# A transformer layer on one core: values of two blocks by seven block products, rope sums partly on GpSimd

## The reference

```python
qkv = x @ w_qkv.T                      # 4096 x 512 by 512 x 1536
q, k, v = split(qkv)                   # 16 heads of 32
q = q * cos + rotate_half(q) * sin
k = k * cos + rotate_half(k) * sin
scores = q @ k.T * 32 ** -0.5          # keep 0 <= row - column < 64
x = layernorm(x + softmax(scores) @ v @ w_out.T)
gate = silu((x @ w_gate) * s_gate)
up = (x @ w_up) * s_up
x = layernorm(x + ((gate * up) @ w_down) * s_down)
```

## Time and profile before

| | |
|---|---|
| median of three runs | 1167.06 (1166.32 to 1167.65) |
| the profiled execution | 1166.03 |
| its span, first to last instruction | 1164.2 |
| PE busy | 1154.0 (99%) |
| DVE busy | 984.6 (85%) |
| ACT busy | 584.4 (50%) |
| POOL busy | 587.3 (50%) |
| DMA: packets, MB | 352077, 134.80 |
| granted TensorE clock | 1.000 of full speed |

### The profile page before, as it was taken

The page is one execution under the profiler, slowest core; times in us unless marked ns, Lnnn a source line. Parts: engine busy times, 40 slices in busy tenths (PEclk is TensorE's granted clock), DMA queues, the critical chain, the costliest instruction groups (busy, mean ns, idle before and its releaser), DMA issues.

```text
span 1164.2 us, 25539 instructions
## 1 busy us (share of the span) xinstructions
PE 1154.0 (99%) x8433; PEld 567.9 (49%) x8433; DVE 984.6 (85%) x2821; ACT 584.4 (50%) x1640; POOL 587.3 (50%) x563
## 2 busy tenths in 40 slices
PE   9999999999999999999999999999999999999998
PEld 4344446444464444644455444554445444464444
DVE  7899998898987899879998899897898988986434
ACT  3953883048820588105880169701686027950330
POOL 0775684156731667326771367613676236752330
PEclk9999999999999999999999999999999999999999
DMA  9999786366562765617656096561964537734000
GB/s 295 173 175 252 137 166 160 66 88 137 111 149 55 110 131 107 145 41 128 132 97 141 37 146 119 101 132 46 155 123 88 131 63 137 120 73 109 19 2 36
DMA packets 352077, 134.80 MB, mean 116 GB/s; under 512 B 309840, under 2 KB 332496, under 8 KB 351952
## 3 DMA queue, kind: packets, MB, share of 16 engines
q1 hardware_dynamic: 334976, 106.86, 49.6%
q0 software_dynamic: 10560, 17.30, 5.1%
q10 hardware_dynamic: 6416, 9.00, 2.1%
HBM read 32.19 MB, written 8.39 MB: 35 GB/s over the span
## 4 chain that ended last, share of the span: by engine, by line
PE 97%; DVE 1%; ACT 1%; issue 1%; POOL 0%; POOLq 0%; DVEq 0%
PE bank L842 61%; PE bank L1058 18%; PE bank L848 10%; PE bank L984 3%; PE bank L964 2%; PE bank L864 1%; PE bank L1080 1%; ACT bank L1243 1%; PE bank L873 0%; PE bank L1069 0%; PE bank L948 0%; DVE wd L1373 0%; ACT wu L1186 0%; DVE ffn_tmp L1530 0%; ACT fuse L1186 0%
## 5 line engine op out<-in xcount | busy, mean ns | idle before, releaser
L842 PE MATMUL bank<-x1T,wg 128*128 128x512 f16 (+1 forms) x1032 | 242.5, 378 | 0.0
L842 PE MATMUL bank<-x1T,wu 128*128 128x512 f16 x1024 | 241.9, 379 | 0.0
L1243 ACT ACTIVATE bank<-bank,neg_max,qk_scale 128x128 f32<-128x128 f32 x512 | 220.5, 435 | 7.8 <-DVE neg_max L1558 6.1
L1058 PE MATMUL bank<-wd,fuse 128*128 128x512 f16 (+2 forms) x1056 | 222.7, 373 | 0.0
L660 POOL TENSOR_TENSOR fuse<-ffn_tmp,fuse 128x512 f16<-128x512 f32 x128 | 149.7, 1170 | 117.5 <-ACT fuse L1186 116.8
L742 POOL TENSOR_TENSOR fuse<-fuse 128x512 f16<-128x512 f32 x116 | 137.7, 1218 | 74.9 <-ACT fuse L1186 72.8
L1058 PEld LDWEIGHTS bank<-wd,fuse 128*128 128x128 f16 x1056 | 101.9, 98 | 118.0
L842 PEld LDWEIGHTS bank<-x1T,wu 128*128 128x128 f16 x1024 | 100.1, 98 | 120.7
L655 POOL TENSOR_TENSOR xT_sb<-probs,xT_sb 128x512 f16<-128x512 f32 x112 | 129.6, 1158 | 44.5 <-ACT xT_sb L1186 44.4
L842 PEld LDWEIGHTS bank<-x1T,wg 128*128 128x128 f16 x1032 | 96.3, 98 | 113.9 <-issue 4.0
L1196 ACT ACTIVATE ffn_tmp<-bank,tanh_scale 128x512 f32<-128x512 f32 x128 | 88.2, 689 | 100.0 <-PE bank L842 76.8
(11 more groups left out here) (235 smaller groups left out, 1621.5 us busy)
## 6 DMA issues: line engine op xcount, KB each, us to landing
v_cross<-v_own SPq DMA_DIRECT2D x64, 128.0 KB, 2.4
out<-x ACTq DMA_DIRECT2D x31, 256.0 KB, 2.0
xT_sb<-xT SPq DMA_DIRECT2D x30, 256.0 KB, 4.1
qkT<-x SPq DMA_DIRECT2D x28, 256.0 KB, 3.8
wg<-w_gate POOLq DMA_DIRECT2D x7, 1024.0 KB, 5.2
wu<-w_up POOLq DMA_DIRECT2D x7, 512.0 KB, 6.0
wqkv<-w_qkvT SPq DMA_DIRECT2D x8, 256.0 KB, 6.3
wg<-w_gate POOLq DMA_DIRECT2D x1, 2048.0 KB, 8.4
```

The lines of the kernel that those rows point to most:

```text
L842: last = pe.matmul(dst, lhsT, rhs, start=(i == 0), stop=(i == len(pairs) - 1))
L1058: last = pe.matmul(dst[:, cols], fuse[:, s, z, rows], wd[:, s, cols], start=(s == 0 and z == 0), stop=(s == STEPS - 1 and z == 1))
L1243: last = act.activation(unit, unit, ACT.Exp, bias=neg_max[:, s % 2, h // 3, h % 3:h % 3 + 1], scale=qk_scale[:, 2:3], accum_out=row_sum[:, ...
```

## The change

1. **Values of blocks 0 and 1 as a pair.** `project_v_pair` computes them with seven products of 128 rows by 256 columns over half of the inner width each, between `down(f, 2)` and `down(f, 3)`. It uses PSUM banks 4, 6, 3 and 1 and the sums of x that the first pair uses too. In the six transitions the two calls of `project_v` for these blocks go. POOL sums the weights for it (`add_v_weights`, four instructions) into the columns that held `added_out`; `reload_columns` is moved behind the pair. DVE adds the products (`sum_v`, seven instructions of 256 columns) between two blocks of the second layernorm, ACT keeps the first product and the high halves in front of stores (`keep_v_first`, `keep_v_pair`), DVE the low ones (`split_v_pair`). The third of the seven products of the first `project_pair` waits for `v_low` of block 1.
2. **DVE order.** `start_y` of block 1 stands ahead of `next_scales`; `carry_keys` and `start_tables` are made earlier; `rope_products` of block 1 stand ahead of the first sum of the second pair.
3. **Rope sums.** Those of blocks 0, 1 and 3 are made by POOL; those of block 2 stay on DVE, with an added wait for `rope_done` of block 1.
4. **ACT order.** `split_high` of block 3 stands behind the exponentials of unit 1. In the prologue the values of block 1 of tile 1, and their halves, are made at its end instead of at the head of the first body.

```diff
+            def project_v_pair(a):
...
+                wait(proj_read, pe, a - 1, NB - 1)
+                done(v_product, quarter(front_left, front_low, low_left))
+                wait(x_summed, pe, a - 1, 3)
+                wait(v_weights_added, pe, a - 2, 3)
+                done(v_product, quarter(back_right, sums[:, 2, :, :], added_out(2)))
+                wait(v_first_kept, pe, a - 2, 0)
+                done(v_product, quarter(front_left, front_high, high_left))
+                done(v_product, quarter(back_left, sums[:, 1, :, :], added_out(1)))
+                done(v_product, quarter(front_right, sums[:, 0, :, :], added_out(0)))
+                wait(v_summed, pe, a - 2, V_SUM_SECOND)
+                done(v_product, quarter(back_left, back_high, added_out(3)))
+                wait(v_summed, pe, a - 2, V_SUM_FOURTH)
+                done(v_done, quarter(front_right, sums[:, 3, :, :], high_right), 2)
...
+                if i == 0:
+                    wait(v_low, pe, a, 1)
                 done(fifth_product, quarter(front_odd, sums[:, 0, :, :], odd_less_even))
...
                 if attn:
-                    project_v(a, 1, ffn)
                     project_v(a, 2, ffn)
                     scores(a, 0, ffn)
                     scores(a, 1, ffn)
...
                     down(f, j, attn)
                     if more and j == 1:
                         spread_maximum(a)
+                    if more and j == 2:
+                        project_v_pair(a + 1)
                 if more:
                     for i in range(2):
                         project_pair(a + 1, i)
-                    project_v(a + 1, 0, ffn)
...
                 rope_products(a, 2 * i, True, range(2, 4), paired=True)
-                rope_sums(a, 2 * i, True)
-                if i == 0:
+                if i:
+                    wait(rope_done, dve, a, 1)
+                    rope_sums(a, 2 * i, True)
+                else:
                     sum_back_even(a, i)
```

More of the change, by code:

```diff
@@ L817, in body @@
                         invert_deviation1(a, j)
-                        if j == 1:
-                            reload_columns(a)
+                        if j == 1 and not more:
+                            reload_columns(a, more)
+                    if more:
+                        add_v_weights(a + 1)
                 for j in range(NB):
@@ L1216, in keep_v, with keep_v_first, keep_v_pair @@
                                   v_scale[:, 1:2]))
+            def keep_v_first(a):
+                wait(v_product, act, a - 2, O_FIRST)
+                wait(ln2_chain, act, a - 2, 4 * 1)
+                done(v_first_kept, copy(v_kept_products()[0], v_places()[0]))
+            def keep_v_pair(a):
+                wait(proj_done, act, a - 1, 1)
+                for place, half, summed in V_HALVES:
+                    wait(v_summed, act, a - 2, summed)
+                    heads = slice(half * HEADS // 2, (half + 1) * HEADS // 2)
+                    last = copy(v_own[:, place // 2, heads, 0, :], v_places()[place].rearrange("p (h d) -> p h d", d=HEAD_DIM),
+                                v_scale[:, 1:2])
+                    if half:
+                        done(v_high, last)
             def carry_v(a):
@@ L1290, in first @@
                     split_x1_high(a, j, ffn)
+                for j in range(2):
+                    keep_v(a + 1, j, True)
             def body(t, attn, ffn, more):
@@ new lines, in split_v_pair @@
+            def split_v_pair(a):
+                for place, half, summed in V_HALVES:
+                    j = place // 2
+                    heads = slice(half * HEADS // 2, (half + 1) * HEADS // 2)
+                    wait(v_high, dve, a, j)
+                    last = dve.scalar_tensor_tensor(out=v_own[:, j, heads, 1, :],
+                                                    in0=v_places()[place].rearrange("p (h d) -> p h d", d=HEAD_DIM),
+                                                    scalar=v_scale[:, 1:2], in1=v_own[:, j, heads, 0, :],
+                                                    op0=ALU.mult, op1=ALU.subtract)
+                    if half:
+                        done(v_low, last)
@@ L1812, in first @@
                 rope_back(a + 1, 1)
-                rope_sums(a + 1, NB - 1, True)
+                for j in range(2):
+                    split_v(a + 1, j, True)
             def front(t, more, attn=True):
@@ L1817, in front @@
                 if attn:
-                    for j in range(2):
-                        split_v(a, j, ffn)
                     for s in range(2):
```

108 lines of the change are left out of this document (91 added, 17 removed).

## The result

The changed kernel takes 1209.64 us (median of 6 runs, 1208.13 to 1210.59) against 1166.97 of the kernel before beside it (6 runs, 1166.32 to 1167.85): a ratio of 1.0364, 95% interval 1.0354 to 1.0375. The forecast was 1184.6, within 1174 to 1191. The sign was right; the size was not, and the time lies outside the range. The profiled execution took 1209.64 (span 1207.8), 43.6 more than the 1166.0 of the one before. From here on T is, as in the prediction, the end of the second pair.

A forecast was written before the change was run, and what follows sets the result against it. The prediction took PE as the bound, busy for all 141.92 us of a steady body. A 3.85 us wait less 0.7 saved gave +3.1 in each of six transitions, +18.6 on 1166.0: 1184.6 us, range 1174 to 1191.

The forecast's parts named there:

- Part 1: PE's saving on values: the new pair takes 6.15 us instead of 6.87, 0.7 saved per transition, 4.3 in six.
- Part 3: End of the second pair: PE waits for block 3's rope products, so unit 1's scores start at T+7.6, 3.85 us late.
- both of its chains: Before unit 1's scores: DVE's rope sums and products to T+7.3; POOL's low halves, then products, to T+6.7 to T+7.6.
- Net per transition: +3.85-0.7: Each of six transitions: the wait at unit 1's scores less the saved value products, +3.1 us.
- a row in which PE is idle for 3 to 4 us: Expected sign in front of unit 1's scores, put down to DVE's rope products, in six transitions and not the prologue.
- Part 2: The value pair's own inputs, between blocks of `down`, and `v_low` for the first pair: cost 0, up to 0.4 us.
- no idle PE at the first pair: Expected sign that the value pair's inputs and `v_low` cost nothing: PE does not wait at the first pair.
- under 7: Copies, splits and one layernorm end before `v_low` of block 1, due some 10 us after the value pair's end.
- The prologue keeps its products and their order: 0: In the prologue, PE's products and their order are unchanged, so nothing is saved there: 0 us.
- The premise: Steady bodies, PE busy all 141.92 us: a product removed saves its full length unless something hidden comes due.
- Rival 4: A second wait later: POOL 1.5 us late, PE waits about 1 us more at the weighted values, 1190.6 us; chance 0.08.
- the rope chain's bounds: Before unit 1's scores: low, DVE undisturbed at T+5.8, 1174.7 us; high, T+8.1 with 0.4 at `down`, 1191.2 us.

The follow-up runs named there:

- e1: The changed kernel with all rope sums moved back from GpSimd to VectorE, the value pair kept: 1214.0 us, ratio 1.0396.
- e4: The changed kernel with four unused 512-column products between the scores of units 0 and 1 in each body: 1210.0 us, ratio 1.0367.
- e11: The changed kernel with eight unused 128x512 products between block 2's values and unit 0's scores in each of seven bodies: 1227.53 us, ratio 1.0517.
- e6: The changed kernel without GpSimd's four sums of value weights, all waits kept (values not the reference's): 1202.94 us, ratio 1.0307.
- e5: The changed kernel with VectorE finishing y of block 2 and splitting the value pair ahead of its loop branch: 1207.16 us, ratio 1.0335.
- e2: The kernel before with only the rope sums of blocks 0, 1 and 3 moved to GpSimd, no value pair: 1178.81 us, ratio 1.0113.
- e3: The changed kernel with block 3's values on TensorE ahead of the scores of units 0 and 1 instead of behind: 1210.76 us, ratio 1.038.
- e8: e3 with ScalarE and GpSimd making the first unit's probability halves ahead of block 3's query and key halves: 1202.65 us, ratio 1.0306.
- e7: The kernel before with the bodies' values of blocks 0 and 1 cut to one of four products (values not the reference's): 1155.35 us, ratio 0.9897.

## Why the prediction failed, point by point

**Part 1 held.** The value pair took 6.13 us (predicted 6.15), the saving is 0.74 a transition.

**Part 3's wait held, by both of its chains.** Unit 1's scores start at T+7.76 (predicted 7.6), and 22.9 us of waiting in all answer to 23.1. GpSimd's low halves of block 1 end at 410.91, T+4.8 (predicted 4.1 to 5.0), and VectorE's two contended sums take 3.0 from start to start (predicted 2.7). VectorE's chain ends last, at 413.85: that is T+7.7, where the prediction had worked out T+7.3 and then took T+7.5, in view of GpSimd's chain. So 0.2 us of the agreement are luck:

```profile
408.34 1.56 DVE L1469 TENSOR_TENSOR fuse<-fuse 128x512 f32<-128x512 f32 x1
409.82 1.64 DVE L1470 TENSOR_TENSOR fuse<-fuse 128x512 f32<-128x512 f32 x1
411.38 2.47 DVE L1462 TENSOR_TENSOR fuse<-bank,tables 128x512 f32<-128x512 f32 x4
```

The pair that took 1.8 before (392.59 to 394.40) takes 3.0 here, beside GpSimd's low halves of block 1, so the two engines hold each other up as in the rows before. e1 shows that this isn't what sets the time, however: without GpSimd in the rope sums, the idle time moved on and did not shrink.

**Part 3's price was the first mis-sized term.** "Net per transition: +3.85-0.7" prices the wait by its own length. It costs 14.5 us more, because the products behind it run at half clock. In the profile before, PE never stood longer than 1 us once its matmuls were running, so nothing in it showed this price. But a row in which PE is idle for 3 to 4 us was my own forecast, and the sum had no term, nor the range a bound, for what comes behind it. e4 and e11 show the term by taking it away: 92.4 us for the same 200 records instead of 105.3. The Trainium skill (TensorE: Matmul & The Clock Gate, Part 1: The HAM clock gate) says that the array's clock goes down to 1.2 GHz when TensorE is idle and up to 2.4 GHz when it is busy again; the rows above agree, with a granted clock of 0.50 behind the stand.

**Part 2, "I cost all this at 0", was the second.** It is some 1.3 us a transition, 7.1 in all, and the sign that the prediction named for this part, no idle PE at the first pair, failed. GpSimd's additions did hold up VectorE, more than the 0.4 that I allowed as an upper bound (0.57 at `down`, e6). And the steps between the value pair and the first pair's third product were summed as instructions, "under 7", without the end of VectorE's loop body among them, where it stands 4.78 us (e5). In the trace before, VectorE was idle for 3.27 us at the end of its loop body, by the profile for PE's `down`, and PE waited for nothing behind it; the change puts PE's wait for `v_low` behind this place.

**"The prologue keeps its products and their order: 0" was the third.** PE's order is kept, but GpSimd's isn't: the sums of block 1 that it takes over stand ahead of what ScalarE needs for the second pair (e2 has the three waits, e1 has none). It is 2.3 of the 2.8 us.

**The premise was too simple.** "A product taken away shortens the run by its full length, as long as nothing that was hidden comes due" is true, but only the first thing that comes due went into the sum. Two things do. Rope and halves keep unit 1's scores back to T+7.8 in the changed kernel, e3 and e8. From there to unit 1's weighted values it takes 18.8 to 20.2 us (e8, e3, e4) where PE waits for them. That is 27 to 28 us in all, for which PE has 22.4. e7 shows the same kind of limit in the kernel before; how much of the second part is ScalarE's new order is not shown (e11). Rival 4 named this second wait, with a chance of 0.08, as an addition to the first. The runs show that it stands in for the first. Where the wait at the scores was filled by work of the kernel, all of it and more came due later (e3: 20.5 gone, 24.7 new at gates and weighted values); where it was filled by unused products, a third did (e4: 20.0 gone, 6.6 new). In the changed kernel it is hidden behind the wait and the low clock, so it is no part of the miss, but it is why none of the mendings brought the time back.

**The range** was built from the rope chain's bounds alone. With the three terms that were set to 0 left without an upper bound, it could not hold.

## What to carry to other kernels

When a product is moved away from a stretch, its time there was also cover for a chain on the other engines: add up that chain to the *last* consumer in the stretch and compare it with the work that TensorE has left, not only the first wait that shows. If the sum forecasts a wait of several us on TensorE, add a term for the clock behind it (here 14.5 us for 22.9 of waiting). And every term that is set to nothing needs a bound of its own: read what its cover is, down to the ends of loops and what other engines do beside it.

## What the hardware showed that I had not expected

- TensorE's granted clock fell from 1.00 to 0.50 across a stand of 3.3 us and was back at 1.00 some 6 us after work went on. In the six transitions the row of the eight 128x512 fp32 products behind such a stand reads 5.39 to 6.57 us instead of 3.70. All in all 22.9 us of waits at the scores cost 37.4, 1.6 times their length.
- A stand of 2.96 us was followed by a gate product of 3.11 us from start to start (e3), one of 1.94 by one of 1.74 (e8).
- VectorE stood 4.78 us at the end of its loop body in one transition and 2.68 in e5, where the instruction behind it was another. It was in no sum of instructions.
- Two splits of x1 on VectorE took 3.43 us beside GpSimd's additions and 1.47 without them. The additions, 1.27 each alone, took up to 1.71 beside them.
